# Causal attention with a fused MLP: value products one per half step, row maxima turned by VectorE, output sums copied in halves

## The reference

```python
scores = jnp.einsum('bhqd,bhkd->bhqk', qh, kh) * scale      # 16 heads of 16, causal
probs = jax.nn.softmax(jnp.where(causal, scores, -jnp.inf), axis=-1)
out = jnp.einsum('bhqk,bhkd->bhqd', probs, vh)
x = x + out.transpose(0, 2, 1, 3).reshape(B, S, D) @ W_proj + b_proj
h = bitlinear(ln(x), w_fc) + gate * (ln(x) @ v.T @ fast_b.T @ u.T)   # w_fc, w_proj ternary
x = x + bitlinear(relu(h) ** 2, w_proj)
```

## Time and profile before

| | |
|---|---|
| median of 3 runs (lowest, highest) | 2110.08 us (2105.65, 2115.99) |
| the profiled execution | 2109.09 us, its span 2107.4 us |
| busy share of the span | PE 96%, DVE 88%, ACT 71%, POOL 23% |
| TensorE clock granted, mean over the span | 0.981 |

### The profile page before, as it was taken

How to read it: one execution, slowest core, us unless ns; L and a number is a source line. 1 busy time by engine, 2 the same in 40 slices (tenths; PEclk the granted TensorE clock), 3 DMA queues, 4 the chain that set the end, 5 groups by cost and what they waited for, 6 DMA issues and landing times. The chain is left out here.

```text
span 2107.4 us, 46575 instructions
## 1 busy us (share of the span) xinstructions
PE 2033.5 (96%) x18225; PEld 1126.7 (53%) x18225; DVE 1854.7 (88%) x3143; ACT 1486.4 (71%) x2787; POOL 475.0 (23%) x637
## 2 busy tenths in 40 slices
PE   6987999999999999999999999999999989999998
PEld 5875444444444444444444444444444458888887
DVE  7988799999999999999999999999999738998996
ACT  2331388888888888888888888888888665555554
POOL 0000011011111111111011111101111127776774
PEclk9997799999999999999999999999999999999999
DMA  6896021121212112122121212212122122323320
GB/s 194 319 324 221 14 71 47 53 58 38 76 46 67 48 48 65 36 77 51 54 58 38 66 47 70 48 53 58 38 76 67 47 74 80 98 86 91 84 77 31
DMA packets 163004, 168.31 MB, mean 80 GB/s; under 512 B 74704, under 2 KB 102880, under 8 KB 162784
## 3 DMA queue, kind: packets, MB, share of 16 engines
q1 hardware_dynamic: 155072, 157.92, 25.9%
q10 hardware_dynamic: 7712, 7.41, 1.2%
HBM read 95.77 MB, written 67.63 MB: 78 GB/s over the span
## 5 line engine op out<-in xcount | busy, mean ns | idle before, releaser
L1021 ACT ACTIVATE probs<-ps_s 128x512 f32<-128x512 f32 x2176 | 1178.7, 596 | 243.2 <-PE ps_s L1211 215.6
L1047 DVE TENSOR_REDUCE maxes<-ps_m 128x2 f32<-128x1024 f32 (+1 forms) x960 | 1142.7, 1220 | 104.9 <-PE ps_m L1174 82.5
L1232 PE MATMUL ps_acc<-probs,vs 128*32 128x256 f32 (+1 forms) x8696 | 694.6, 391 | 11.2 <-ACT acc_sb L999 11.2
L1211 PE MATMUL ps_s<-qs,ks 50*128 50x512 f32 (+3 forms) x2560 | 571.1, 444 | 0.8 <-ACT probs L1021 0.7
L1174 PE MATMUL ps_m<-ks,qs 48*128 48x512 f32 (+3 forms) x2560 | 498.7, 388 | 13.7 <-DVE maxes L1047 8.3
L1211 PEld LDWEIGHTS ps_s<-qs,ks 50*128 50x128 f32 x2560 | 251.4, 183 | 408.4 <-ACT probs L1021 373.4
L1232 PEld LDWEIGHTS ps_acc<-probs,vs 128*32 128x32 f32 x8696 | 172.8, 108 | 290.3 <-issue 188.9
L953 POOL TENSOR_SCALAR_AFFINE_SELECT probs<-probs 128x512 f32<-128x512 f32 x256 | 158.8, 635 | 721.9 <-ACT probs L1021 718.0
L1174 PEld LDWEIGHTS ps_m<-ks,qs 48*128 48x128 f32 x2560 | 260.9, 189 | 90.5 <-DVE maxes L1047 70.9
L1054 DVE CUSTOM_DVE_ANT_0 sums_masked<-ps_m,mask 128x384 f32<-128x384 f32 (+1 forms) x512 | 186.6, 420 | 21.7 <-PE ps_m L1174 5.7
L1425 POOL TENSOR_TENSOR hid<-square,hid 128x512 fp32r<-128x512 f32 x128 | 175.4, 1382 | 97.6 <-DVE square L1436 85.7
(11 more groups left out here) (133 smaller groups left out, 1851.0 us busy)
## 6 DMA issues: line engine op xcount, KB each, us to landing
qs<-q_scr SPq DMA_DIRECT2D x384, 64.0 KB, 2.7
ks<-k_scr SPq DMA_DIRECT2D x384, 64.0 KB, 2.8
q_scr<-probs SPq DMA_DIRECT2D x32, 512.0 KB, 3.9
k_scr<-probs SPq DMA_DIRECT2D x32, 512.0 KB, 5.3
o_scr<-acc_sb SPq DMA_DIRECT2D x64, 256.0 KB, 2.9
v_scr<-probs SPq DMA_DIRECT2D x16, 512.0 KB, 6.0
v_dense<-v_scr SPq DMA_DIRECT2D x16, 512.0 KB, 4.5
o_in<-o_scr SPq DMA_DIRECT2D x32, 256.0 KB
```

What stands on the lines that cost most here:

```text
L1021: act.activation(probs[:, s % RING, x], ps_s[:, k % BANKS], ACT.Exp).then_inc(ring_taken, 1)
L1047: last = dve.tensor_reduce(maxes[c % 2][:, :, pairs, tt, i], banks, AX.X, ALU.max)
L1211: last = pe.matmul(ps_s[:, k % BANKS, at:at + width], ks[u][rows, j // TT, p, j % TT * P:(j % TT + 1) * P], qs[u][rows, c, p, q0:q0 + widt ...
L1232: last = pe.matmul(ps_acc[h * VW:(h + 1) * VW, q0:q0 + width], vs[u][:, j, h], probs[:, s % RING, h % banks_of(s), at:at + width], start=( ...
```

## The change

- `order`: every half step has exactly one entry of value products, that of six half steps before (`VALUES_BEHIND`), counted over both kinds of steps; `halves_of` cuts a diagonal step's 384 + 128 columns into 256 and 128 + 128.
- `turn_rows` moves from TensorE, ScalarE and the ring to VectorE: one `dve.transpose`, which turns blocks of 32x32. `max_rows` is now 128x32, and the row DMAs go block by block: 8 of 2 KB for each chunk in the place of 4 of 4 KB. SP waits for VectorE (`rows_turned`).
- `vector_masks`: the 512-wide diagonal items too are masked and reduced by VectorE, and their mask matmuls go; the 256-wide pairs keep theirs. The mask tile grows from 384 to 512 columns.
- the sums are copied in two halves of 256 columns: the first one half step before the last value product, which waits for that copy; the next chunk waits for both.

```diff
+VALUES_BEHIND = 6
-def vector_masks(pieces):
-    return pieces[0][4] != pieces[-1][4]
+def vector_masks(c, pieces):
+    return pieces[0][2] == c and pieces[0][4] != 2 * P
...
-    if len(blocks) > 1:
-        return [blocks[:1], blocks[1:]]
-    return [[(j, q0, col, width // 2)], [(j, q0 + width // 2, col + width // 2, width // 2)]]
+    return [[(j, q0, col, 2 * P)], [(j, q0 + 2 * P, col + 2 * P, width - 2 * P)] + blocks[1:]]
+VALUES = [(s, halves) for s in range(NS) for halves in ([(0,), (1,)] if banks_of(s) == 4 else [(0, 1)])]
 def order(s, last):
-    x = sum(banks_of(i) // 2 for i in range(s))
-    if banks_of(s) == 4:
-        got = [("bank", 0), ("bank", 1), *items_at(x), ("values", (0,)), ("bank", 2), ("bank", 3), *items_at(x + 1), ("values", (1,))]
-    else:
-        got = [("bank", 0), ("bank", 1), ("values", (0, 1)), *items_at(x)]
+    got = []
+    for half in range(banks_of(s) // 2):
+        x = sum(banks_of(i) // 2 for i in range(s)) + half
+        y = x - VALUES_BEHIND
+        got += [("bank", 2 * half), ("bank", 2 * half + 1), *items_at(x), ("values", (y < 0, *VALUES[y % len(VALUES)]))]
+def acc_piece(s, halves):
+    if 1 not in halves:
+        return None
+    return 1 if s + 1 in CHUNK_END else 0 if s + 2 in CHUNK_END else None
...
+            def store_rows(n, u, c):
+                sp.wait_ge(rows_turned, NCH * n + c + 1)
+                for i in range(P // TURN):
+                    for r in range(2):
+                        dst = qs[u][ROW * r + TERMS:ROW * r + TERMS + MROWS, c].rearrange("a p (t i q) -> a (p t) i q", i=P // TURN, q=TURN)[:, :, i]
+                        row = TURN * i + r * MROWS * PAIRS * TT
+                        sp.dma_start(dst.bitcast(F32), max_rows[c % 2][row:row + MROWS * PAIRS * TT, :].bitcast(F32)).then_inc(rows_in[c % 2], 16)
...
-                act.copy(lead.acc_sb[c % 2][:], ps_acc[:]).then_inc(acc_copied, 1)
+                part = slice(2 * P * piece, 2 * P * (piece + 1))
+                act.copy(lead.acc_sb[c % 2][:, part], ps_acc[:, part]).then_inc(acc_copied, 1)
...
+            def turn_rows(n, c):
+                dve.wait_ge(max_parted, 2 * (NCH * n + c + 1))
+                if not early(n, c):
+                    dve.wait_ge(rows_in[c % 2], 16 * ROWS * halves(n, c))
+                dve.transpose(max_rows[c % 2][:].bitcast(F32),
+                              max_parts[c % 2][:].bitcast(F32).rearrange("p r a x -> p (r a x)")).then_inc(rows_turned, 1)
...
-                    pe.wait_ge(rows_in[c % 2], 16 * 2 * MROWS * (halves(n, c) + 1))
+                    pe.wait_ge(rows_in[c % 2], 16 * ROWS * (halves(n, c) + 1))
...
-                        pe.wait_ge(acc_copied, NCH * n + c)
+                        pe.wait_ge(acc_copied, 2 * (NCH * n + c))
+                    if s + 1 in CHUNK_END:
+                        pe.wait_ge(acc_copied, 2 * (NCH * n + c) + 1)
```

More of the change, by code:

```diff
@@ L839, in taken @@
         def taken(n, k):
-            return OPENED_ROWS + USES * n + k + 1
+            return USES * n + k + 1
         def scores_taken(n, s, last):
-            kinds = [(what, x) for what, x in order(s, last) if what in ("bank", "rows")]
+            kinds = [(what, x) for what, x in order(s, last) if what == "bank"]
             return taken(n, ring_uses(s, last) + kinds.index(("bank", banks_of(s) - 1)))
@@ L892, in body @@
                         if what == "rows":
-                            store_rows(*unit_of(x, n, u)[1:], taken(n, k))
-                        k += what in ("bank", "rows")
+                            store_rows(*unit_of(x, n, u))
                     if at := ended(s, PV_BEHIND + 1, n, first):
@@ L984, in _, with copy_acc @@
             load_ones(act, sh, ks[1])
[L986 to L997, removed]
-                    act.wait_ge(lead.sums_in[c % 2], 16 * GH * halves(n, c))
-                act.copy(lead.acc_sb[c % 2][:], ps_acc[:]).then_inc(acc_copied, 1)
[L1001 to L1005, removed]
+            def copy_acc(n, s, piece):
+                c = STEPS[s][0]
+                act.wait_ge(pv_done, NS * n + s + 1)
+                if piece == 0 and not early(n, c):
+                    act.wait_ge(lead.acc_stored[c % 2], 16 * halves(n, c))
+                    act.wait_ge(lead.sums_in[c % 2], 16 * GH * halves(n, c))
+                part = slice(2 * P * piece, 2 * P * (piece + 1))
+                act.copy(lead.acc_sb[c % 2][:, part], ps_acc[:, part]).then_inc(acc_copied, 1)
             def body(n, u, first, last):
@@ L1022, in body @@
                             k += 1
[L1023 to L1028, removed]
+                        elif what == "values" and not (first and x[0]):
+                            if (piece := acc_piece(*x[1:])) is not None:
+                                copy_acc(n - 1 if x[0] else n, x[1], piece)
                     if last and s == O_HIGH_AT:
@@ L1135, in body @@
                             find_max(unit, c)
+                        elif what == "rows":
+                            unit, _, c = unit_of(x, n, u)
+                            turn_rows(unit, c)
                     if at := ended(s, PV_BEHIND + 6, n, first):
@@ L1174, in form_max @@
                         last = pe.matmul(ps_m[:, 2 * slot + r, col:col + width], qs[par][rows, c, p, tt * P:(tt + 1) * P],
-                                         ks[par][rows, i, p, 0:width], start=True, stop=(i < c or vector_masks(pieces)), skip_group_check=True)
-                    if i == c and not vector_masks(pieces):
+                                         ks[par][rows, i, p, 0:width], start=True, stop=(i < c or vector_masks(c, pieces)), skip_group_check=True)
+                    if i == c and not vector_masks(c, pieces):
                         for half in range(2):
@@ L1299, in body @@
                             form_max(*unit_of(x, n, u))
-                        elif what == "rows":
-                            unit, _, c = unit_of(x, n, u)
-                            await_bank(n, k, first)
-                            turn_rows(unit, c, k)
-                            k += 1
-                        elif what == "values" and s >= PV_BEHIND:
-                            values(n, u, s - PV_BEHIND, x, last)
+                        elif what == "values" and not x[0]:
+                            values(n, u, *x[1:], last)
                         elif what == "values" and not first:
-                            values(n - 1, 1 - u, NS + s - PV_BEHIND, x, False)
+                            values(n - 1, 1 - u, *x[1:], False)
                         elif what == "values":
```

73 lines of the change are left out of this document (29 added, 44 removed).

## The result

The kernel after takes 2321.19 us (median of 4 runs, 2291.19 to 2347.27) where the kernel before takes 2110.63 (4 runs): ratio 1.095, 95% interval 1.084 to 1.106. It was forecast slower, at 2163 us with a range up to 2198; it is 158 us slower than that.

The account below looks back on a forecast made before the run. TensorE was taken to set the pace, with SP's queue full: 2109.1 + 36 (queue) + 15.5 (last unit's wait) + 2 (clock) - 1.4 (savings) + 1 (opening) = 2162, median 2163 us, range 2112 to 2198.

Parts of the forecast that it names:

- Direction and mechanism: Whole kernel: TensorE sets the pace, SP's queue has no room before half step 46; slower by over 0.5%, chance 0.76.
- The queue: SP's row DMAs, 0.68 us an issue, delay half steps 39 and 46: unit 93.2 us, +36 us in all; chance 0.5.
- The rivals of a cheap issue: Row DMAs in SP's queue: at 0.47 us each 2111, no change, chance 0.13; at 0.34 faster, 2080, chance 0.11.
- The last unit: Chunk 3's rows are turned behind step 16's ternary work on VectorE; TensorE stands still 15.5 us at half step 39.
- the clock's: Last unit only: 2 us of slow matmuls (0 to 3.4) added for the 15.5 us wait.
- the rival: Clock falls in every unit at the waits of half steps 39 and 46: 1.6 us a unit, 2187; chance 0.22.
- the argument against the rival: Between the waits at half steps 39 and 46 TensorE is busy all the time, unlike where the price was read.
- The unit without the queue: One unit by TensorE's own time, leaving out SP's queue: 87.8 us, 3.0 less than now.
- Masks: 512-wide diagonal items: TensorE saves 1.1 us a unit, VectorE pays +2.6, TensorE waits some 0.9 in half steps 23-32.
- Turn: Turned rows leave TensorE, ScalarE and the ring: 0.8 us a unit saved; VectorE's new instruction takes 0.2 each.
- Value products and halves: Even spacing removes most of a unit's 3.4 us of waits not for sums; half copies cost 1.3, about as before.
- The opening: 40 items ahead of the first scores, most of them paced by VectorE: +1 us.

Follow-up runs that it names:

- run 6: Kernel before, turn kept on TensorE, each of its four row DMAs cut in two so SP issues eight: 2343.73 us, ratio 1.098.
- run 1: Kernel after with useless matmuls, 5 ahead of the wait at half step 39 and 10 ahead of that at half step 46: 2214.85 us, ratio 1.037.
- run 7: Kernel after with the last unit's ternary work on VectorE one step later, 17 for 16: 2278.4 us, ratio 1.076.
- run 11: run 5 with one stand of TensorE of varied length, made by GpSimd fills, in each of units 1 to 14: 2118.3 us.
- run 12: run 5 with two stands of TensorE, 0.96 and 2.63 us, in each of units 1 to 14: 2284.0 us, ratio 1.082.
- run 5: Kernel after with rows turned three half steps earlier and stack loads reordered in SP's queue by due times: 2074.84 us, ratio 0.982.
- run 8: Kernel before with only the masks of the 512-wide diagonal items moved to VectorE: 2125.8 us, ratio 1.005.
- run 3: Kernel after in all but the turn, which stays on TensorE and ScalarE with 4 row DMAs: 2097.11 us, ratio 0.990.
- run 9: Kernel before with only value products one per half step and sums copied in halves: 2087.33 us, ratio 0.990.
- run 10: run 5 with the masks of the 512-wide diagonal items back on TensorE: 2062.8 us, ratio 0.977.

## Why the prediction was wrong, and where it was right

- **Direction and mechanism: right.** TensorE is the bound, SP's queue had no slack at half step 46, and the doubled row DMAs break it (run 6 shows it with nothing else changed).
- **The queue: right.** Issue 0.68 taken, 0.66 measured; turn 0.2, 0.20; first row DMA +2.8, +2.7; rows landed +9.3, +9.2; item of half step 46 +22.45, +22.1; wait at half step 39 1.9, 1.57; unit 93.2, 93.1 (93.0 to 94.0 in run 1). Of the mask matmuls 512 are gone, the 128 groups forecast. The rule that an issue is small beside its DMA (the Trainium skill, DMA: Bandwidth & Descriptors, Issuing engines are not separate DMA queues) does not carry this kernel: four more issues cost it 2.7 us at a due time (5.50 us for 2.78, run 6). The rivals of a cheap issue fall with it.
- **The last unit: right.** 15.5 us forecast, 15.31 measured; run 7 takes it away by moving VectorE's work by a step.
- **The step that failed is the clock's.** The sum holds 2 us for it, in the last unit, and the rival prices a fall at "1.6 us", "that price a unit, once", 24 us in all. In units 1 to 14 alone it cost 143 us, 10 a unit. Two errors: the price came from a window of 5 us in a place where the clock rose again after 6.8 us (1718.8 to 1725.6), while here it stayed low for 3.4 to 54.6 us; and the argument against the rival ("between those waits TensorE is busy all the time") is no protection, since TensorE was busy for 54.51 of 54.60 us at 1.2 GHz. Unit 0 took 20.6 us more than before where the forecast had 2.4, the last unit 19.4 where it had 16.1, and the queue cost 30.4 in fourteen units where it had 33.6. From the profiled execution, which the sum gave as 2162: 2162 + 143 + 18 + 3 - 3 = 2323, against 2324 measured. The rival should have led, with an upper end far above 2198. That a wait for a DMA ahead of a stretch of matmuls brings the clock down each time anew is told by the Trainium skill (TensorE: Matmul & The Clock Gate, HAM oscillation — how this bites in real kernels); runs 11 and 12 agree in part: a stand of TensorE brought the clock down in 4 units of 14 and in 14 of 14. But it is not each time: the waits of 1.57 to 1.60 us at half step 39 of the kernel after did it in 10 units of 14.
- **The unit without the queue: the sum right by luck, its terms not.** 87.8 forecast, 87.9 to 88.3 measured (run 5). The forecast put -0.3 to the masks, -0.8 to the turn and -1.9 to the value products and halves; the runs give +0.1, -1.7 and -1.1, and the errors cancel. *Masks*: -1.1 forecast with up to 0.9 of waits against it, +0.55 measured alone (run 8), +0.1 beside the rest (runs 3 and 9, 5 and 10). The item's price was right (0.61 us between the instructions, 1.46 from item to item), but it is longer than the half step of 1.38 us whose masks it replaces, so VectorE sets the pace there (run 8). VectorE in the kernel after:

```profile
1326.87 0.69 DVE L1052 CUSTOM_DVE_ANT_0 sums_masked<-ps_m,mask 128x512 f32<-128x512 f32 x1
...
1327.49 0.69 DVE L1052 CUSTOM_DVE_ANT_0 sums_masked<-ps_m,mask 128x512 f32<-128x512 f32 x1
...
1328.33 0.56 DVE L1052 CUSTOM_DVE_ANT_0 sums_masked<-ps_m,mask 128x384 f32<-128x384 f32 x1
```

*Turn*: 0.8 taken, 1.7 measured (89.5 in run 9 to 87.8 in run 10, with no wait for a DMA in either; run 10 has the rows and stacks earlier too, which was not tried apart). The forecast took the half step with the turn alone, 1.44 for 1.24, not what follows it in the ring: half steps 33 to 39, with two turns in them, take 8.25 us in run 9 and 7.50 in run 10, and nearly all of that lies in half steps 33 to 35: 1.55, 1.44 and 1.45 us for 1.23 each. *Value products and halves*: 90.65 to 89.5, -1.1 (run 9).
- **The opening**: +1 forecast, +1.5 up to unit 0, but unit 0 ran 45.4 us at half clock. In the profiles with the 512-wide masks on VectorE the opening's low clock reached over 20 us into unit 0 in four of nine (after, runs 1, 5, 8), and in two more (runs 7, 11) it rose at the end of the opening and fell again within 5 us of unit 0's start, for 85.3 and 54.6 us, behind a wait of 0.7 us. In those with the masks on TensorE neither came in any of five. That VectorE's longer items cause it was not tried by itself.

## What to carry to other kernels

A queue of DMAs has due times like an engine: before a change adds issues, list what stands behind them and when it is waited for, and order the loads by that. And price a new wait of TensorE not by its length but with the clock: here waits of 1.6 us or more, one or two in a unit, cost some ten more in matmuls at 1.2 GHz. Where such a wait can't be avoided, fill it with matmuls that nobody reads: that kept the clock up in 11 of 14 units of run 1.

## What the runs showed of the hardware that was not expected

- In units 1 to 14 of all the profiles together, every one of the 59 stands of TensorE of 1.74 to 4.78 us was followed by a fall to 1.2 GHz, for 3.4 to 64.9 us, the longest with TensorE busy in all of it (run 12); of the 36 from 1.41 to 1.72 us 24 were, and of the 46 from 0.66 to 1.36 none. No run showed what sets how long a fall lasts, or which of the stands in the middle bring one.
- A stand is not the only thing ahead of a fall. The kernel before has one of 3.4 us at 1674.4, with TensorE busy for 12.00 of the 12.00 us ahead of it, and runs 7 and 11 have those of unit 0 told above. What brings these about stays open.
- A us at half clock cost the kernel after 0.36 us, not 0.5. Part of the rest lies in a wait that would have come anyway: where the clock fell at half step 39, TensorE came late to half step 46 and found k there. Where it fell at half step 46 (units 4, 9, 13), a us cost 0.43 to 0.47, counted from unit 10's 93.07 us. What hides the last bit was not followed up.
- In unit 10 the clock fell at half step 39 and cost nothing: TensorE came to half step 46 1.5 us later than in units 1, 4, 9 and 13, and waited 1.72 us there for their 3.3 to 4.6.
- Cutting a 4 KB DMA in two doubles the time of its issue: 8 x 0.69 us for 4 x 0.70. Bytes and pieces hardly count.
